# Vision transformer block with routed experts, one core: choosing two experts per token by VectorE's MAX and MAX_INDEX

## The reference, cut to what matters

```python
h = patches @ W_emb + b_emb, with two class tokens in front, + pos   # 16 images x 38 tokens x 192
h = h + attention(layernorm(h))            # local, strided and anchored linear attention, 12 heads
y = layernorm(h)                           # 608 tokens
logits = y @ Wg                            # 8 experts
probs = softmax(logits)
topv, topi = top_k(probs, 2)               # the earlier expert wins a tie
cw = topv / sum(topv)
h = h + sum_k cw[k] * (relu(y @ W1[topi[k]] + b1) @ W2[topi[k]] + b2)
```

## Time and profile before

| | |
|---|---|
| median of 3 runs | 270.45 us (267.88 to 270.51) |
| the profiled execution, its own time | 268.69 us |
| its span, first to last instruction | 266.9 us |
| PE busy | 223.2 us (84%) |
| DVE busy | 150.5 us (56%), 464 instructions |
| ACT busy | 110.5 us (41%) |
| POOL busy | 73.7 us (28%) |
| mean granted TensorE clock | 0.855 of 2.4 GHz |

### The profile page before, as it was taken

The page is one execution under the profiler, slowest core; times in us unless marked ns, Lnnn a source line. Parts: engine busy times, 40 slices in busy tenths (PEclk is TensorE's granted clock), DMA queues, the critical chain, the costliest instruction groups (busy, mean ns, idle before and its releaser), DMA issues.

```text
span 266.9 us, 4475 instructions
## 1 busy us (share of the span) xinstructions
PE 223.2 (84%) x1340; PEld 191.6 (72%) x1340; DVE 150.5 (56%) x464; ACT 110.5 (41%) x252; POOL 73.7 (28%) x103
## 2 busy tenths in 40 slices
PE   6379699796999999998989955189999999999950
PEld 6268399564697967876767752079999999999940
DVE  5234318859476957858575688756768443433300
ACT  2343463767133453726242478035433342424210
POOL 4001260073305050414221335001324242423330
PEclk9658659799799999999985555559999999999995
DMA  7999999999400000000101298351333334341213
GB/s 121 132 233 172 235 287 271 266 225 289 123 10 0 0 4 1 2 0 0 29 2 26 56 324 205 80 136 42 70 47 59 47 54 52 52 55 18 29 15 85
DMA packets 26259, 25.73 MB, mean 96 GB/s; under 512 B 4970, under 2 KB 23261, under 8 KB 26221
## 3 DMA queue, kind: packets, MB, share of 16 engines
q1 hardware_dynamic: 22333, 22.16, 35.1%
q0 software_dynamic: 3568, 2.64, 7.8%
q10 hardware_dynamic: 336, 0.66, 1.7%
HBM read 16.56 MB, written 7.77 MB: 91 GB/s over the span
## 4 chain that ended last, share of the span: by engine, by line
PE 62%; DVE 14%; DMA 11%; issue 4%; ACT 3%; POOL 2%; SPq 2%; DVEq 0%; POOLq 0%; ACTq 0%
PE ps L950 11%; PE ps L973 10%; PE ps L580 5%; PE ps L708 4%; DMA wemb<-in_L_tok_W_emb 4%; DMA sums<-ys,xs 4%; PE ps L798 4%; PE ps L712 4%; PE ps L784 4%; PE ps L677 3%; PE ps L962 3%; PE ps L691 2%; DMA sent<-row,index 2%; SPq L428 1%; POOL sent L1612 1%
## 5 line engine op out<-in xcount | busy, mean ns | idle before, releaser
L1648 POOL DMA_INDIRECT sums<-ys,xs x17 | 26.3, 1546 | 67.0 <-ACT ys L1548 60.7
L973 PE MATMUL ps<-w2s,hidT 128*128 x204 | 36.1, 327 | 1.1 <-DVE hidT L1352 0.8
L973 PEld LDWEIGHTS ps<-w2s,hidT 128*128 128x128 f32 x204 | 33.2, 189 | 2.0 <-issue 1.6
L950 PE MATMUL ps<-w1hi,xhi 128*128 x68 | 25.3, 372 | 1.4 <-DVE xhi L1332 0.8
L1548 ACT ACTIVATE ys<-ps,xs 128x192 f32<-128x192 f32 x17 | 7.2, 421 | 40.0 <-PE ps L973 37.6
L1331 DVE TENSOR_TENSOR xlo<-ps,xhi 128x128 fp32r<-128x128 f32 x17 | 5.0, 292 | 29.8 <-ACT xend L1541 29.8
L784 PE MATMUL ps<-vm,ktok 114*96 114x288 f32 (+1 forms) x48 | 15.6, 406 | 5.0 <-DVE kvb L1147 5.0
L1635 POOL COPY vexp<-vtok 114x32 f32<-114x32 f32 (+1 forms) x36 | 8.0, 222 | 41.4 <-PE ps L712 39.5
L1430 ACT ACTIVATE qlb<-ps,cst 96x228 f32<-96x228 f32 (+1 forms) x36 | 12.1, 425 | 17.2 <-PE ps L746 17.2
L1612 POOL DMA_INDIRECT sent<-row,index x12 | 13.5, 1128 | 18.1 <-DVE row L1219 14.8
L708 PE MATMUL ps<-at,vexp 114*96 114x114 f32 (+1 forms) x144 | 18.2, 281 | 0.0
(11 more groups left out here) (197 smaller groups left out, 486.3 us busy)
## 6 DMA issues: line engine op xcount, KB each, us to landing
w2s<-in_L_ffn_W SPq DMA_DIRECT2D x8, 576.0 KB, 8.0
sent<-blank SPq DMA_DIRECT2D x1, 3977.0 KB, 32.3
w1s<-in_L_ffn_W SPq DMA_DIRECT2D x4, 768.0 KB, 17.1
xs<-sent SPq DMA_DIRECT2D x17, 96.0 KB, 1.9
w1s<-in_L_ffn_W SPq DMA_DIRECT2D x4, 384.0 KB, 18.5
w1hi<-w1hi SPq DMA_DIRECT2D x8, 192.0 KB, 3.9
ximg<-in_x SPq DMA_DIRECT2D x12, 96.0 KB, 9.3
w1s<-in_L_ffn_b SPq DMA_DIRECT2D x1, 792.0 KB
```

What stands on the lines that cost most here:

```text
L950: last = pe.matmul(ps[2 + c][:, 0:PASS], xx, of_expert(ww, expert), start=(n == 0), stop=(n == len(products) - 1))
L973: last = pe.matmul(ps[6 + j % 2][:, 0:D], hidT[:, k, :], of_expert(w2s[:, :, k, :], expert), start=(k == 0), stop=(k == FCH - 1))
L1648: po.indirect_dma_start(sums, bass.IndirectOffsetOnAxis(ap=xs[:, j % NS, D + TAIL + 1:].bitcast(U32), axis=0), ys[:, j % 2, :], None, comp ...
```

## The change

route no longer compares pairs. VectorE's MAX writes the eight logits in falling order into `top`, MAX_INDEX their positions into `topi`, one comparison with a new constant `order` (0 to 7) makes `sel`, and the sum of its two halves is `both`. The difference of the first two of `top` replaces the product, the sum and the difference. send lets the sum write the row numbers straight as integers into `index`, and no longer writes the token number: GpSimd writes it for all groups once, at its start. The wait for the difference's completion at the end of route goes too; the wait for `run` stands behind the difference.

```diff
@@ route(g)
-                ve.wait_ge(dv_logits, g + 1)
-                t0, n, _ = group(g)
-                mine = pair[0:n, g, 0, :].unsqueeze(2).broadcast_to([n, E, E])
-                other = pair[0:n, g, 0, :].unsqueeze(1).broadcast_to([n, E, E])
-
-                link(ve.tensor_tensor(cmpa[0:n], other, mine, ALU.is_equal))
-                link(ve.tensor_tensor(cmpb[0:n], cmpa[0:n], tri[0:n].rearrange("p (a b) -> p a b", a=E), ALU.mult))
-                link(ve.tensor_tensor(cmpa[0:n], other, mine, ALU.is_gt))
-                link(ve.tensor_tensor(cmpb[0:n], cmpb[0:n], cmpa[0:n], ALU.add))
-                link(ve.tensor_reduce(rank[0:n], cmpb[0:n], AX.X, ALU.add))
-                ve.tensor_scalar(both[0:n, g, :], rank[0:n], float(TOP), None, ALU.is_lt).then_inc(dv_both, 1)
-                for k in range(TOP):
-                    link(ve.tensor_scalar(sel[0:n, g, k, :], rank[0:n], float(k), None, ALU.is_equal))
+                n = group(g)[1]
+                ve.wait_ge(dv_logits, g + 1)
+                link(ve.max(top[0:n, g, :], logit[0:n, g, :]))
+                link(ve.max_index(topi[0:n, g, :], top[0:n, g, :], logit[0:n, g, :]))
+                link(ve.tensor_tensor(sel[0:n, g], topi[0:n, g, 0:TOP].unsqueeze(2).broadcast_to([n, TOP, E]),
+                                      const("order")[0:n, :].unsqueeze(1).broadcast_to([n, TOP, E]), ALU.is_equal))
+                ve.tensor_tensor(both[0:n, g, :], sel[0:n, g, 0, :], sel[0:n, g, 1, :], ALU.add).then_inc(dv_both, 1)
                 ve.wait_ge(dv_both, 2 * g + 1)
                 ve.tensor_tensor(run[:, g + 1, :], run[:, g, :], both[:, g, :], ALU.add).then_inc(dv_both, 1)
+                ve.tensor_tensor(diff[0:n, g, 0:1], top[0:n, g, 1:2], top[0:n, g, 0:1], ALU.subtract).then_inc(dv_diff, 1)
                 ve.wait_ge(dv_both, 2 * g + 2)
-                link(ve.tensor_tensor(pick[0:n], sel[0:n, g], pair[0:n, g, 0:1, :].broadcast_to([n, TOP, E]), ALU.mult))
-                link(ve.tensor_reduce(best[0:n, g, :], pick[0:n], AX.X, ALU.add))
-                ve.tensor_tensor(diff[0:n, g, 0:1], best[0:n, g, 1:2], best[0:n, g, 0:1], ALU.subtract).then_inc(dv_diff, 1)
-                ve.wait_ge(dv_diff, g + 1)
@@ send(g)
-                link(ve.tensor_tensor(pick[0:n], sel[0:n, g], pair[0:n, g, 1:2, :].broadcast_to([n, TOP, E]), ALU.mult))
-                link(ve.tensor_reduce(place[0:n, :], pick[0:n], AX.X, ALU.add))
-                link(ve.tensor_copy(index[0:n, g, :], place[0:n, :]))
+                link(ve.tensor_tensor(pick[0:n], sel[0:n, g], slot[0:n, g, :].unsqueeze(1).broadcast_to([n, TOP, E]), ALU.mult))
+                with nc.allow_low_precision(reason="row numbers: whole, one term of each sum is not zero"):
+                    link(ve.tensor_reduce(index[0:n, g, :], pick[0:n], AX.X, ALU.add))
...
-                link(ve.tensor_tensor(row[0:n, g, 1, D:D + 1], row[0:n, g, 0, D:D + 1], diff[0:n, g, 1:2], ALU.mult))
-                ve.tensor_copy(row[0:n, g, :, D + 1].bitcast(U32),
-                               const("number")[0:n, g:g + 1].broadcast_to([n, TOP])).then_inc(dv_row, 1)
+                ve.tensor_tensor(row[0:n, g, 1, D:D + 1], row[0:n, g, 0, D:D + 1], diff[0:n, g, 1:2], ALU.mult).then_inc(dv_row, 1)
@@ gpsimd, ahead of the loop
             link(po.tensor_copy(own[:], const("expert")), gp_own)
+            for g in range(GROUPS):
+                link(po.tensor_copy(row[:, g, :, D + 1].bitcast(U32),
+                                    const("number")[0:GTOK, g:g + 1].broadcast_to([GTOK, TOP])))
             link(po.memset(both[:], 0.0), gp_route_zero)
```

More of the change, by code:

```diff
@@ L90 @@
     "tri": (GTOK, E * E),
+    "order": (GTOK, E),
     "before": (GTOK, GTOK),
@@ L131, in constants @@
     put("tri", np.broadcast_to((e[:, None] > e[None, :])[None], (GTOK, E, E)))
+    put("order", np.broadcast_to(e, (GTOK, E)))
     put("before", j < s)
@@ L180, in build @@
         comb = sb("comb", [GTOK, GROUPS, E])
[L181 to L184, removed]
+        logit = sb("logit", [GTOK, GROUPS, E])
+        slot = sb("slot", [GTOK, GROUPS, E])
+        top = sb("top", [GTOK, GROUPS, E])
+        topi = sb("topi", [GTOK, GROUPS, E], U32)
         sel = sb("sel", [GTOK, GROUPS, TOP, E])
@@ L188, in build @@
         pick = sb("pick", [GTOK, TOP, E])
-        best = sb("best", [GTOK, GROUPS, TOP])
-        place = sb("place", [GTOK, TOP])
         index = sb("index", [GTOK, GROUPS, TOP], U32)
@@ L1175, in take_logits @@
                 ve.wait_ge(pe_logits, g + 1)
-                ve.tensor_copy(pair[0:n, g, 0, :], ps[1][0:n, 256:256 + E]).then_inc(dv_logits, 1)
+                ve.tensor_copy(logit[0:n, g, :], ps[1][0:n, 256:256 + E]).then_inc(dv_logits, 1)
             def take_places(g):
@@ L1181, in take_places @@
                 ve.wait_ge(pe_places, g + 1)
-                ve.tensor_tensor(pair[0:n, g, 1, :], ps[4][0:n, 0:E], const("region")[0:n, :], ALU.add).then_inc(dv_places, 1)
+                ve.tensor_tensor(slot[0:n, g, :], ps[4][0:n, 0:E], const("region")[0:n, :], ALU.add).then_inc(dv_places, 1)
             def route(g):
+                n = group(g)[1]
                 ve.wait_ge(dv_logits, g + 1)
-                t0, n, _ = group(g)
-                mine = pair[0:n, g, 0, :].unsqueeze(2).broadcast_to([n, E, E])
```

## The result

The changed kernel takes 257.25 us (median of 4 executions, 256.42 to 259.32), the kernel before beside it 270.06 us (267.88 to 270.51): a ratio of 0.955, 95% interval 0.947 to 0.963, so 12.8 us less. The forecast was 262.1 us with a range of 259.2 to 266.3; the kernel is 2 us faster than that range holds. This ratio and all that follow leave out executions more than 1.5% above the fastest of their kernel, which for the kernel before is a good part of them, so medians over all executions stand beside them. The profiled execution took 256.9 us, span 255.1 us, against 268.69 and 266.9.

What follows compares the result with a forecast made beforehand. Bound by PE's matmuls, its waits for VectorE's route and send, the halved clock and VectorE's tail before the last scatters; 1.09 + 1.29 + 1.51 + 0.9 + 2.7 = 7.5 us off 269.6 gave 262.1 us, range 259.2 to 266.3.

Steps and rivals of the forecast that it cites:

- Durations: VectorE's route and send: route 1.2 us against 2.58, send 0.42 us less, GpSimd's casts hidden.
- Rival 4: Index search in the six routes is slow; at 2 us more per route, 271.9 us; chance 3%.
- Pauses, clock and step 9: PE's waits in steps 7 and 8 (1.09, 1.29), full clock behind them (1.51), step 9's earlier `run` of group 3 (0.9).
- The tail: From route(4) to the last scatter: shorter VectorE work and earlier cT and places(5) start that scatter 2.7 us sooner.
- Rival 3: Weight transfers at 150 to 167 us take the last scatters' 2.7 us gain: 264.8 us; chance 10%.
- the clock term: Part 3 to the end of project_out behind step 8's pause runs at full clock, saving at least 1.51 us.
- the base: Starting time for the gain: 269.6 us, the middle between the profiled execution and the median of 270.45.
- Rival 2: Clock also holds over group 5's outputs, 146.68 to some 152.7 us: 2.1 us more gain, 260.0 us; chance 12%.
- rival 1: Clock falls where it fell, so nothing is gained at half clock: 264.0 us; chance 27%.

Runs made afterwards that it cites:

- e4: Kernel before with the new route only, the old send with its two casts kept and no GpSimd casts: 258.69 us, ratio 0.969 to the kernel before.
- e6: Changed kernel with idle VectorE instructions behind the loop: seven ahead of route(4) and of route(5), two in send(4) and send(5): 262.18 us, ratio 0.973.
- e10: Changed kernel with PE's places(5) moved ahead of output_biases, nothing else: 257.19 us, ratio 0.967 to the kernel before.
- e1: Kernel before with an unused 32-byte-per-partition tensor ahead of the expert weights, shifting later SBUF addresses: 268.05 us, ratio 1.002.
- e9: Kernel before, unchanged, run again for a second profile: 268.46 us.
- e12: Kernel before, unchanged, run again for a third profile: 269.5 us.
- e2: Changed kernel with an unused 224-byte-per-partition tensor, putting later tensors at the kernel before's addresses: 257.59 us, ratio 0.975 to the kernel before.
- e13: Changed kernel with nine idle VectorE instructions behind send in step 7 only: 265.43 us, ratio 0.985 to the kernel before.
- e14: Changed kernel with nine idle VectorE instructions behind send in step 8 only: 262.02 us, ratio 0.970 to the kernel before.
- e5: Changed kernel with nine idle VectorE instructions behind send in both steps 7 and 8: 264.13 us, ratio 0.985 to the kernel before.
- e16: Changed kernel with idle VectorE instructions in steps 7 and 8, ahead of route(3), route(4) and route(5), and in send(4) and send(5): 267.08 us.
- e7: Changed kernel with places(5) ahead of output_biases and ten PE matmuls on constants ahead of the first tile: 260.26 us.
- e3: Kernel before with the new send only (integer sum, token numbers by GpSimd) and the old pair ranking: 264.83 us, ratio 0.999.
- e15: Changed kernel with nine idle VectorE instructions in both steps 7 and 8, measured a second time: 264.89 us, ratio 0.982 to the kernel before.
- e11: Changed kernel, unchanged, measured a third time: 258.45 us, ratio 0.972 to the kernel before.

## Why the forecast was wrong

By its own steps, in the recorded pair:

- **Durations: right.** MAX took 0.19 us (0.21 forecast) and MAX_INDEX 0.28 (0.30); the integer sum is free, the difference and GpSimd's casts are hidden. The Trainium skill's Vector Engine (DVE) Microarchitecture Reference, section 3.9, has the search as two instructions, and the trace agrees: MATCH_VALUE_LOAD 0.09 us and FIND_INDEX8 0.16. But two instructions together cost what I gave to one, not one step more, since the first is half a step. Rival 4 (a slow search) needed 1.5 us more per route and is out.
- **Pauses, clock and step 9: right in kind.** 1.09 + 1.29 + 1.51 + 0.9 = 4.79 forecast, 3.94 measured. The clock held over project_out(4), as said, and fell behind it, at 135 us; but it fell with PE busy without a break, and not at two waits for VectorE, as the forecast had it. What I didn't have is a short stretch at half speed inside step 8; it cost 1.7 us (1.97 + 2.48 against 1.42 + 1.34). e4's profile hasn't got it and gains 5.70 us there (44.59 to 38.89).
- **The tail: right.** 2.66 against 2.7, with cT, places(5) and the last scatter in the places named, and e6 confirms it by putting them back. Rival 3 (the transfers take the gain) didn't come true here, the last landing was 0.54 us shorter; in e10 it did for 0.7 us.
- **The step that failed: the clock term, 1.51 us, read from one execution of the kernel before.** That execution had kept its clock in steps 7 and 8. The forecast saw that it "may hold a lucky clock", but moved only the base for it, by 0.9 us, and left the gain. The base was right: 269.6 against 270.06 us measured. The gain was not. In three further profiles of the kernel before (e1, e9, e12) route(0) to residual(5) takes 49.1 to 49.7 us, not 44.59. Against e9 and e12 (49.05) the changed kernel gains 8.4 us there, of which the two pauses and step 9 are 3.3 and the clock some 5, not 1.51. The luck was hidden by a late head: 108.17 us to route(0) against 104.1 to 105.5. In the time of the kernel before the two nearly cancel; in the recorded pair, where the clock gives little, the same microseconds show up as 4.63 us of head. The recorded pair's 7.1 us come near the 7.5 forecast because both stand on that one execution, and 0.54 of them is a shorter landing, which the forecast didn't have.
- **What these 5 us are made of.** In e9 and e12 the clock is at half for 3 us at 112 to 116 us (1.7 us lost), for 7 us behind the pause of step 7 (3.4 lost), and from the pause of step 8 on (1.5 lost); the changed kernel loses 1.7 in step 8. e13 and e14 show by edits that the pauses of steps 7 and 8 cost more than their length. The first 1.7 us lie ahead of both pauses, and e2, with the new route, loses them too: that they are the change's is not shown. Rival 2, "the clock holds longer", had the right sign, but put the gain behind step 8, where nothing was won. What was won lies in steps 7 and 8.

With that, 8.4 to residual(5), 2.7 for the tail and 0.7 for the landing (4.2 to 3.4 or 3.7) make 11.8 us. Measured side by side, the medians of the two kernels differ by 12.8, 9.7 and 10.4 us, and by 8.9 with e2 for the changed one. From 269.6 us, 11.8 less is 258. But the three further profiles are of executions of 269.5 to 270.7 us; of 48 executions of the kernel before ten took 263.2 to 266.6 us, and none of those was profiled. So 49.1 us is what its slower executions do, and 11.8 is high rather than typical.

The forecast disagreed with the Trainium skill, TensorE: Matmul & The Clock Gate, section HAM oscillation — how this bites in real kernels, by which only a longer pause lets the clock fall. By that rule the time would have been rival 1's 264.0 us. The runs bear the forecast out: waits of 0.94 us in e13, 1.09 in e12 and 1.15 in e5 are each followed by half speed within 2 to 4 us, and the changed kernel's clock falls there with no wait but 0.54 us for the residual.

**What stays open.** What decides on a fall isn't shown, and a pause is not the whole rule: the recorded execution of before and that of e16 had the step-7 pause and kept the clock, and in e7 it was at half for 10 us with no pause of that part at all. The half-speed stretch at 112 to 116 us came in e1, e3, e9, e12, e15 and, at 110 to 114 us, in e2, with the old route and the new; in e9 and e12 the rows of PE ahead of it agree to 0.01 us in time, counted from route(0), with those of the recorded execution, which kept its clock. So what decides is not in PE's rows just ahead. Nor is it tested why the head varies (103.1 to 108.2 us over 18 profiles); in the recorded pair it goes with the first weights' landing and the clock at 30 to 40 us, 0.53 before and 0.87 after. And nothing here explains the landing of the last scatter, which makes 2.9 us of e13's cost.

## What to carry to other kernels

A pause of one microsecond in a dense stretch of TensorE's work can cost several times its length, as in e13: price it by putting it back into the faster kernel, not by its length. One profile is one draw of the clock. Where a time of 270 us spreads by 7 us without a change, take several profiles of the kernel before and compare stretch by stretch between rows that both have, since a late head can hide a lucky clock. And where the profiled execution may have had a lucky clock, correct the gain for it, and not only the time that it is taken from.

## What had not been expected of the hardware

- VectorE's MAX and MAX_INDEX on 114 x 8 take 0.16 and 0.09 + 0.16 us: a top two of eight with positions in 0.47 us from start to start.
- A single wait of 0.94 us in step 7 raised the median to 265.4 us (e13), from the changed kernel's 257.3 to 258.5.
- TensorE's clock falls to half in a stretch where PE is busy without a break: 4.00 of 4 us at 124 to 128 us in the changed kernel, mean clock 0.59, with one wait of 0.54 us some 2 us ahead.
- The last scatter lands in 3.36 to 6.21 us. The load beside it doesn't sort the cases: over the landing itself the DMA share is 0.55 in e13 (6.21 us) and 0.71 in e11 (3.36 us).
